# A transformer block on one core: all softmax denominators of the second half's queries summed on GpSimd, and the ones product of the sum as a step of its own

## The chip, the cores and the metric

The kernel runs on one core of one Trainium2 chip. The metric is the device time of one execution in microseconds. Engines are named as in the profile: PE is TensorE's matmul side and PEld its weight loads, DVE is VectorE, ACT is ScalarE, POOL is GpSimd, SP is SyncE, which here issues all transfers.

## What is computed

Input x is 4 batches of 1024 tokens with 128 features, all float32. Three layers follow each other:

```python
x = x + 0.5 * ffn(layernorm(x))      # 8 experts of 128x128, the two best by a router, weighted
x = x + attention(layernorm(x))
x = x + 0.5 * ffn(layernorm(x))

# attention: 8 query heads of 128, 2 key/value heads (4 query heads share one), causal
q = (x @ wq).reshape(B, T, 2, 4, 128)
k_lat, v_lat = x @ wk_down, x @ wv_down        # 32 wide for each key/value head
k, v = k_lat @ wk_up, v_lat @ wv_up
scores = q.k * 128**-0.5, masked to key <= query
y = softmax(scores) @ v
return y.reshape(B, T, 1024) @ wo
```

## The kernel before

**Tiling.** A batch has two chunks of 512 tokens (c = 0, 1) and eight tiles of 128 (j = 0 to 7). The attention works in *quads*: one chunk of queries and one key/value head g with its four query heads. There are 16 quads in all, Q = 4b + 2c + g. A quad with c = 0 has key tiles 0 to 3, one with c = 1 (the second half's queries) has key tiles 0 to 7. The up projections of keys and values are folded into the queries and into `wo`, so keys and values are 32 wide.

**The steps of a quad.** (1) `maximum` (M): scores in the query by key layout, from which VectorE takes each query's maximum (`reduce`), merged, transposed (R) and added to the stacked queries as two rows by SP's transfers. (2) `scores` (S): for each of the quad's *slots* (26 of 512 columns where c = 1, 10 where c = 0) the scores in key by query layout, the causal squares masked by a small bf16 product; two banks take turns. (3) `exponent` (E, on ACT, L739) turns the bank into weights in `prob`, a ring of 16 slots. (4) `weighted_values` (V, L1257): one step for each key tile, four heads, each onto 32 partitions of the bank OB, f32 (two matmul instructions each, so eight in the trace). (5) The denominators: the same weights times `ones` [128 x 32] (L1262) into a second bank.

**Widths.** Where key tile j lies on the diagonal (j >= 4c), only queries from `first_query(q, j)` = (j - 4c) * 128 on see it. So for c = 1 tiles 0 to 4 are 512 queries wide, tile 5 is 384, tile 6 is 256 and tile 7 is 128. Tiles 5 and 7 share four slots (384 + 128 columns), and tile 6 has two slots with two heads each. `ORDER[q]` gives the tiles in the order in which their weights come: 0, 1, 2, 3, 4, 5, 7, 6.

**Who sums what.** In c = 1 quads the tiles of `summed(q)`, 0 to 4, have no ones product of their own. GpSimd adds their weights into `sums` (`add_weights`, L620): for each pair of heads, tile 1 to tile 0, then tiles 2, 3, 4 onto it, eight adds of 2 x 512 elements a partition. The tiles of `direct(q)`, 5 to 7, and all tiles of c = 0 quads get ones products on PE. The last values step (tile 6) waits for the quad's adds and does the ones product of `sums` as well (L1268), into the same bank. A slot of `prob` may be overwritten when its values step is done and, for summed tiles, its add too (`exponent`).

**After a quad.** VectorE transposes the denominators, takes the reciprocal and spreads it (`denominators`, L995 to L1002); ACT copies OB to `o_sb` (`output`); GpSimd multiplies (`normalise`, L607, POOL's Y); when a chunk's two quads are through, PE multiplies by `wo` (`join`, J, L1279), VectorE adds x, and the layer norm and the last ffn of this chunk can begin. `o_sb`, `r_t` and OB exist once, so quads pass through there one after the other.

**The other work.** The experts (`expert_products`, Y on PE, L1165 to L1167) fill PE between attention steps; ACT and VectorE weigh them (L704, L947) and GpSimd adds up (`finish_tile`, three operations a tile, POOL's F, L591 to L598). GpSimd also takes the layer norm's -0.5 power (L574) and the shift (L578), POOL's N, n and m, each after seven small VectorE operations (`statistics`, L861).

**What sets the order.** Each engine's program is a written list: `PE_ORDER`, `DVE_ORDER`, `ACT_ORDER`, `POOL_ORDER`, `SP_ORDER`, one letter a step. A step waits for its semaphores with everything behind it. A digit behind a PE letter is the PSUM bank that the step takes; `take` waits until the bank's former content has been read. The end of both lists before, for PE and for POOL:

```python
    "Sl7Y0VSSY1SY5SSY6VSSY0SY7SVSSY1SY5SVSSSSSV2VVY3Y2Y6J0JJJz7l1Y0Y5Y2Y3Y6Y7Y1Y0"       # PE
    "FFFFFAAAAAAFAFAFFYmmYYAAAAAAAAmmFFFFFFFFFYFFFFFFAFAFFAAAAAAFFFFFFYFFFFFFmmFFFFFFFFFFFFFFFFFF"   # POOL
```

## Time and profile before

| what | us |
|---|---|
| median of 3 runs (512.12 to 513.83) | 512.28 |
| the profiled execution | 512.54 |
| its span, first to last instruction | 510.8 |
| PE busy | 462.2 |
| DVE busy | 415.8 |
| ACT busy | 336.8 |
| POOL busy | 302.2 |
| mean granted clock of PE, share of full speed | 0.954 |

The profiled execution is 0.26 us above the median, and 1.7 us of it lie around the span. In the profile a matmul's end is modelled and busy times of neighbours overlap, so the time from one start to the next tells better what a step costs PE. A note in brackets behind a timeline row is the idle time of the engine before it and what ended it.

### The profile page before, as it was taken

What the parts mean: (1) busy time and instruction counts of PE and PEld (TensorE: products, weight loads), DVE (VectorE), ACT (ScalarE), POOL (GpSimd) and SP (SyncE); (2) the same over time, 40 slices, a digit from 0 to 9 for tenths busy, and PEclk for the clock granted to TensorE, in tenths of its full rate; (3) what the DMA queues carried; (4) which work ended last, traced back from release to release, by engine and by line L of the source; (5) the groups of instructions that cost most, each with busy time, mean ns of one, the idle gap of its engine ahead of it and who ended that gap; (6) DMA issues with size and microseconds to landing.
All of it is one profiled execution on the core that took longest, in us unless ns stands there. A gap on an engine that the chain in (4) does not pass through costs nothing.

```text
span 510.8 us, 9871 instructions
## 1 busy us (share of the span) xinstructions
PE 462.2 (90%) x3166; PEld 251.1 (49%) x3166; DVE 415.8 (81%) x1320; ACT 336.8 (66%) x748; POOL 302.2 (59%) x323
## 2 busy tenths in 40 slices
PE   1896989998699999999999999999999999899752
PEld 1673535453254446464645664555534545454441
DVE  6787789989976988989969999988888877863454
ACT  3356417667359767797787976677776496788523
POOL 4166006209745940598489737298498129889835
PEclk9995967999889999999999999999999999999967
DMA  7001310002001010002110100210101000000000
GB/s 199 16 22 42 88 48 22 1 2 81 19 2 32 18 33 2 1 1 58 23 57 13 53 1 2 48 33 17 53 2 54 1 1 2 1 23 1 22 21 21
DMA packets 21123, 14.50 MB, mean 28 GB/s; under 512 B 2952, under 2 KB 20944, under 8 KB 21072
## 3 DMA queue, kind: packets, MB, share of 16 engines
q1 hardware_dynamic: 21072, 13.88, 10.6%
q8 instruction: 25, 0.41, 0.3%
q14 instruction: 26, 0.21, 0.2%
HBM read 3.78 MB, written 2.10 MB: 11 GB/s over the span
## 4 chain that ended last, share of the span: by engine, by line
PE 70%; DVE 14%; ACT 6%; issue 5%; POOL 2%; DMA 2%; SPq 1%; ACTq 0%; POOLq 0%; DVEq 0%
PE bank L1257 12%; PE bank L1235 11%; PE bank L1212 11%; PE bank L1165 6%; PE bank L1262 5%; PE bank L1166 5%; PE bank L1167 5%; DVE diff L861 3%; PE bank L1240 2%; PE bank L1183 2%; ACT prob L739 2%; ACT xn L675 2%; PE bank L1279 2%; DMA x<-in_L_attn_x 2%; PE bank L1152 1%
## 5 line engine op out<-in xcount | busy, mean ns | idle before, releaser
L739 ACT ACTIVATE prob<-bank,exp_scale 128x512 f32<-128x512 f32 x288 | 188.6, 690 | 61.2 <-PE bank L1240 33.1
L620 POOL TENSOR_TENSOR sums<-sums,prob 128x1024 f32<-128x1024 f32 x48 | 112.3, 2371 | 9.5 <-ACT prob L739 9.5
L1212 PE MATMUL bank<-k_stack,q_stack 96*128 96x512 f16 (+3 forms) x384 | 101.2, 336 | 8.5 <-DVE m_part L963 5.4
L1235 PE MATMUL bank<-q_stack,k_stack 98*128 98x512 f16 (+3 forms) x384 | 105.3, 330 | 2.0 <-ACT prob L739 1.5
L704 ACT ACTIVATE scaled<-bank,gate 128x128 f32<-128x128 f32 x256 | 75.3, 374 | 28.7 <-POOL x L598 10.5
L591 POOL TENSOR_TENSOR pair_sum<-dve_sum,scaled 128x256 f32<-128x256 f32 x64 | 46.7, 730 | 80.2 <-DVE dve_sum L947 66.7
L967 DVE TENSOR_REDUCE m_part<-bank 128x1 f32<-128x512 f32 x128 | 83.4, 679 | 7.0 <-PE bank L1212 6.4
L963 DVE CUSTOM_DVE_ANT_0 masked<-bank,mask_qk 128x384 f32<-128x384 f32 (+1 forms) x128 | 75.1, 617 | 8.5 <-PE bank L1212 8.3
L1257 PE MATMUL bank<-prob,v_lat 128*32 128x512 f32 (+3 forms) x768 | 81.8, 500 | 0.1
L1165 PE MATMUL bank<-we_hi,xT_hi 128*128 128x512 f32 x128 | 66.8, 522 | 1.6 <-DVE m_part L963 1.6
L1235 PEld LDWEIGHTS bank<-q_stack,k_stack 98*128 98x128 f16 x384 | 33.4, 98 | 64.7 <-ACT prob L739 32.0
L1212 PEld LDWEIGHTS bank<-k_stack,q_stack 96*128 96x128 f16 x384 | 33.6, 100 | 51.9 <-issue 13.5
L1166 PE MATMUL bank<-we_lo,xT_hi 128*128 128x512 f32 x128 | 53.6, 419 | 0.0
L1167 PE MATMUL bank<-we_hi,xT_lo 128*128 128x512 f32 x128 | 53.4, 417 | 0.0
L607 POOL TENSOR_TENSOR yT<-o_sb,r_t 128x512 f32<-128x512 f32 x16 | 20.4, 1277 | 51.8 <-DVE r_t L1002 49.7
L675 ACT ACTIVATE xn<-x,shift,rstd 128x128 f32<-128x128 f32 x96 | 40.8, 489 | 10.6 <-POOL shift L578 10.6
L620 POOL TENSOR_TENSOR sums<-prob 128x1024 f32<-128x1024 f32 x16 | 37.8, 2366 | 13.2 <-ACT prob L739 13.2
L574 POOL TENSOR_TENSOR rstd<-var_eps,half_power 128x4 f32<-128x4 f32 (+1 forms) x18 | 22.0, 1225 | 38.6 <-DVE neg_mean L861 38.6
L947 DVE SCALAR_TENSOR_TENSOR dve_sum<-bank,gate,scaled 128x128 f32<-128x128 f32 x128 | 39.7, 342 | 6.3 <-ACT scaled L704 6.1
L1240 PE MATMUL bank<-mask_kq,ident_b 128*128 128x256 bf16 (+1 forms) x160 | 40.4, 252 | 0.0
L1262 PE MATMUL bank<-prob,ones 128*32 128x384 f32 (+3 forms) x448 | 37.9, 410 | 0.0
L1165 PEld LDWEIGHTS bank<-we_hi,xT_hi 128*128 128x128 f32 x128 | 26.1, 204 | 17.5 <-issue 5.6
(128 smaller groups left out, 722.8 us busy)
## 6 DMA issues: line engine op xcount, KB each, us to landing
q_stack<-q_hi SPq DMA_DIRECT2D x32, 128.0 KB, 3.2
x<-in_L_attn_x SPq DMA_DIRECT2D x8, 256.0 KB, 3.0
q_stack<-q_lo SPq DMA_DIRECT2D x16, 128.0 KB, 3.2
out_x<-x SPq DMA_DIRECT2D x8, 256.0 KB, 2.3
k_stack<-k_hi SPq DMA_DIRECT2D x16, 64.0 KB, 2.1
we<-in_L_ffn_expert_weights SPq DMA_DIRECT2D x1, 512.0 KB, 4.0
x<-in_L_attn_wq SPq DMA_DIRECT2D x1, 512.0 KB, 6.6
x<-in_L_attn_wo SPq DMA_DIRECT2D x1, 512.0 KB, 7.9
```

The costliest lines, as they stand in the source:

```text
L620: nc.gpsimd.tensor_tensor(into, first if j == 1 else into, new, ALU.add).then_inc(sum_step, 1)
L704: nc.scalar.activation(scaled[:, tile % NTB, i, :], home_of(("y", f, n, 2 * t))[:, i * D:(i + 1) * D], ACT.Copy, scale=gate_of(f, n, t)[:, ...
L739: nc.scalar.activation(prob[:, n % NP, :], bank[ST + n % NST][:], ACT.Exp, scale=exp_scale[:, 0:1]).then_inc(p_ready, 1)
L963: V.tensor_tensor_reduce(out=masked[:, m % 2, 0:w], in0=seen[:, 0:w], in1=mask_qk[:, CH - w:CH], op0=ALU.add, op1=ALU.max, scale=1.0, scal ...
L967: V.reduce_max(into, seen[:, 0:w], AX.X).then_inc(mx_red, 1)
L1165: mm(into[:], hi, we_hi[:, cols(half)], start=True, stop=False)
L1166: mm(into[:], hi, we_lo[:, cols(half)], start=False, stop=False)
L1167: mm(into[:], lo, we_hi[:, cols(half)], start=False, stop=True).then_inc(y_done, 1)
L1212: last = mm(into[:, n * w:(n + 1) * w], q_stack[0:MROW, c, g * NR + r, (i % TC) * P:(i % TC + 1) * P], k_stack[0:MROW, b % 2, g, k:k + w], ...
L1235: last = mm(into[:, at:at + CH - off], k_stack[:, b % 2, g, j * P:(j + 1) * P], q_stack[:, c, g * NR + r, off:CH], start=at == 0, stop=not ...
L1257: last = mm(bank[OB][r * DL:(r + 1) * DL, off:CH], v_lat[:, b % 2, j, g, :], weights[r], start=first, stop=final, skip_group_check=True)
L1262: last = mm(sums_to[r * DL:(r + 1) * DL, off:CH], ones[:], weights[r], start=j == direct(q)[0], stop=final and not summed(q), skip_group_c ...
```

## The change

1. `summed(q)` gives all eight tiles of a c = 1 quad, in the order 0, 1, 2, 3, 4, 5, 7, 6; `direct` goes. GpSimd does six adds more in each of these eight quads, two for each of tiles 5, 7 and 6, as narrow as the tile: 2 x 384, 2 x 128 and 2 x 256 elements a partition. The tiles' ones products go: 12 of them a quad, 24 matmul instructions.
2. The ones product of the sum leaves the last values step. It becomes `sum_products`, step D of `PE_ORDER`, takes the denominator bank itself and raises a new semaphore, `den_done`. VectorE's transpose waits for that in c = 1 quads, and the first add of a quad waits for it in the place of `pv_done` before it overwrites `sums`.
3. The weights slots of tiles 5, 6 and 7 are now also held until their adds are done (`exponent` is unchanged but asks `summed`).
4. All five order lists are new. They hold the same steps, but for POOL's 112 A in the place of 64, and PE's eight D.

```diff
 def summed(q):
-    c, g = QUADS[q]
-    return list(range(c * TC + 1)) if c else []
-
-def direct(q):
-    return [j for j in ORDER[q] if j not in summed(q)]
+    return ORDER[q] if QUADS[q][0] else []
+
+def quads_summed(Q):
+    return sum(QUADS[i % NQ][0] for i in range(Q + 1))
...
 def sum_done(b, q, j, pair):
-    return sum_count(b * NQ + q) - 2 * len(summed(q)[1:]) + 2 * (max(j, 1) - 1) + pair + 1
+    return sum_count(b * NQ + q) - 2 * len(summed(q)[1:]) + 2 * (max(summed(q).index(j), 1) - 1) + pair + 1
...
 PE_ORDER = steps(
...
-    "Sl7Y0VSSY1SY5SSY6VSSY0SY7SVSSY1SY5SVSSSSSV2VVY3Y2Y6J0JJJz7l1Y0Y5Y2Y3Y6Y7Y1Y0"
...
+    "M0SM6M5SM1SM7SM0SV6SSVSJ5M1SM7VSM0SVSJSM1VVSR7JSVSSVSSJSSVSSJ0SSJVVSVJSSJSSVSSz6Sz1Y7l5lY0SVY6SSY1SSVSSz5Y7Y"
+    "0SY6SSVSSY1SVY5SSY7SY0SVVY1Y6SY2Y3Y7Vl5Y0D1Y6Y2Y1Y3Y7Y5Y0D6J6JJJz2l1Y6Y3Y5Y7Y0Y2Y1Y6"
 POOL_ORDER = (
...
-    "FFFFFAAAAAAFAFAFFYmmYYAAAAAAAAmmFFFFFFFFFYFFFFFFAFAFFAAAAAAFFFFFFYFFFFFFmmFFFFFFFFFFFFFFFFFF"
...
+    "nAAAAAAAAAAAFAAFFAFFFAFFFFFAFFAAFYFAFAFFAFAAAFAFAFAFFAYYAAAAAAYAmAmAAAAmAAmAAAAFAAFFFFFAFFFFAFFFFFAFAFAFFFAFA"
+    "AYFFFYFFFFFFmmFFFFFFFFFFFFFFFFFF"
...
+    "D": [("den", Q) for Q in range(NB * NQ) if QUADS[Q % NQ][0]],
...
             def add_weights(b, q, j, pair):
-                Q, g = b * NQ + q, QUADS[q][1]
-                heads = slice(2 * pair, 2 * pair + 2)
-                new, first = (prob[:, at % NP:at % NP + 2, :] for at in
-                              (b * NS + QSTART[q] + weights_at(q, i)[2 * pair][0] for i in (j, 0)))
-                into = sums[:, g, heads, :]
-                pool.wait_ge(p_ready, b * NS + QSTART[q] + weights_at(q, j)[2 * pair + 1][0] + 1)
+                g, off = QUADS[q][1], first_query(q, j)
+                slots = [(b * NS + QSTART[q] + i, at) for i, at in weights_at(q, j)[2 * pair:2 * pair + 2]]
+                (one, at), (two, beside) = slots
+                new = prob[:, one % NP:one % NP + 2, at:at + CH - off] if two > one else \
+                    prob[:, one % NP, :].rearrange("p (h q) -> p h q", h=2)
+                first = (b * NS + QSTART[q] + 2 * pair) % NP
+                first = prob[:, first:first + 2, :]
+                into = sums[:, g, 2 * pair:2 * pair + 2, off:CH]
+                pool.wait_ge(p_ready, two + 1)
                 if j == 1 and pair == 0:
-                    need(pool, pv_done, (GROUP[b - 1, q, ORDER[q][-1]] + 1) if b else 0)
+                    need(pool, den_done, quads_summed(b * NQ + q - NQ) if b else 0)
...
                     b, q = divmod(Q, NQ)
-                    dve.wait_ge(pv_done, GROUP[b, q, ORDER[q][-1]] + 1)
+                    if summed(q):
+                        dve.wait_ge(den_done, quads_summed(Q))
+                    else:
+                        dve.wait_ge(pv_done, GROUP[b, q, ORDER[q][-1]] + 1)
...
-                sums_to = take(("den", b * NQ + q)) if j == direct(q)[0] else home_of(("den", b * NQ + q))
-                if j not in summed(q):
+                if not summed(q):
+                    sums_to = take(("den", b * NQ + q)) if first else home_of(("den", b * NQ + q))
                     for r in range(NR):
                         last = mm(sums_to[r * DL:(r + 1) * DL, off:CH], ones[:], weights[r],
-                                  start=j == direct(q)[0],
-                                  stop=final and not summed(q), skip_group_check=True)
-                if final and summed(q):
-                    pe.wait_ge(sum_step, sum_count(b * NQ + q))
-                    for r in range(NR):
-                        last = mm(sums_to[r * DL:(r + 1) * DL, :], ones[:], sums[:, g, r, :],
-                                  start=False, stop=True, skip_group_check=True)
+                                  start=first, stop=final, skip_group_check=True)
                 last.then_inc(pv_done, 1)
+
+            def sum_products(Q):
+
+                into = take(("den", Q))
+                pe.wait_ge(sum_step, sum_count(Q))
+                for r in range(NR):
+                    last = mm(into[r * DL:(r + 1) * DL, :], ones[:], sums[:, Q % NKV, r, :],
+                              start=True, stop=True, skip_group_check=True)
+                last.then_inc(den_done, 1)
```

## Rows read from the trace of the kernel before

**Rows 1.** The page's part 1: busy time, share of the span, instructions.

```profile
PE 462.2 (90%) x3166; PEld 251.1 (49%) x3166; DVE 415.8 (81%) x1320; ACT 336.8 (66%) x748; POOL 302.2 (59%) x323
```

**Rows 2.** Windows: stretch, its length, each engine's busy us, granted clock, DMA share, GB/s.

```profile
118.00:150.00 32.00, 26.27 (x157) 12.28 (x161) 31.15 (x73) 16.50 (x28) 23.09 (x13) 0.89 0.15 39
200.00:300.00 100.00, 99.74 (x700) 55.99 (x698) 87.81 (x287) 80.30 (x186) 73.79 (x77) 1.00 0.11 27
300.00:420.00 120.00, 119.58 (x938) 61.80 (x936) 104.28 (x292) 85.21 (x177) 69.35 (x65) 1.00 0.09 22
422.54:481.04 58.50, 55.51 (x389) 28.69 (x388) 35.67 (x126) 43.55 (x97) 53.98 (x45) 1.00 0.03 7
```

**Rows 3.** Groups by form, GpSimd: count, busy us, mean ns, idle before and its releasers.

```profile
L620 POOL TENSOR_TENSOR sums<-sums,prob 128x1024 f32<-128x1024 f32 x48 | 112.3, 2371 | 9.5 <-ACT prob L739 9.5
L591 POOL TENSOR_TENSOR pair_sum<-dve_sum,scaled 128x256 f32<-128x256 f32 x64 | 46.7, 730 | 80.2 <-DVE dve_sum L947 66.7 <-PE bank L1070 8.7 <-DVE x L1008 4.7
...
L607 POOL TENSOR_TENSOR yT<-o_sb,r_t 128x512 f32<-128x512 f32 x16 | 20.4, 1277 | 51.8 <-DVE r_t L1002 49.7 <-issue 2.1
...
L574 POOL TENSOR_TENSOR rstd<-var_eps,half_power 128x8 f32<-128x8 f32 x6 | 9.8, 1642 | 15.8 <-DVE neg_mean L861 15.8
...
L578 POOL TENSOR_TENSOR shift<-neg_mean,rstd 128x8 f32<-128x8 f32 x6 | 1.2, 204 | 0.5
```

**Rows 4.** Timeline, GpSimd, last two quads: start us, length us, operation, count.

```profile
422.54 4.72 POOL L620 TENSOR_TENSOR sums<-prob 128x1024 f32<-128x1024 f32 x2 [0.36 <-ACT prob L739]
427.21 14.01 POOL L620 TENSOR_TENSOR sums<-sums,prob 128x1024 f32<-128x1024 f32 x6
...
479.76 1.28 POOL L607 TENSOR_TENSOR yT<-o_sb,r_t 128x512 f32<-128x512 f32 x1
```

**Rows 5.** The chain that ended last, from 476 us: start us, length us, piece.

```profile
476.95 0.90 PE bank L1268 x8
...
481.18 2.04 PE bank L1279 x16
```

**Rows 6.** Timeline, PE, end of quad 11: values (L1257) and ones products (L1262, L1268).

```profile
389.18 0.83 PE L1262 MATMUL bank<-prob,ones 128*32 128x384 f32 x8
389.94 0.39 PE L1235 MATMUL bank<-q_stack,k_stack 98*128 98x512 f16 x1
...
392.58 0.40 PE L1262 MATMUL bank<-prob,ones 128*32 128x128 f32 x8
392.92 0.61 PE L1212 MATMUL bank<-k_stack,q_stack 96*128 96x512 f16 x2
...
393.78 0.64 PE L1257 MATMUL bank<-prob,v_lat 128*32 128x256 f32 x8
394.24 0.61 PE L1262 MATMUL bank<-prob,ones 128*32 128x256 f32 x8
394.67 1.04 PE L1268 MATMUL bank<-sums,ones 128*32 128x512 f32 x8
395.64 0.39 PE L1212 MATMUL bank<-k_stack,q_stack 96*128 96x512 f16 x1
```

**Rows 7.** The same chain near 455 us: a 512 wide values step by itself.

```profile
455.48 0.99 PE bank L1257 x8
```

**Rows 8.** Timeline, PE: the scores of quad 14's slot 5.

```profile
420.87 0.39 PE L1235 MATMUL bank<-q_stack,k_stack 98*128 98x512 f16 x1
```

**Rows 9.** VectorE's statistics (min/median/max ns, then timeline rows), and a PE wait.

```profile
L861 DVE TENSOR_TENSOR diff<-stats x18: 153/166/2283, 6.8 to 485.1; 128x4 f32<-128x4 f32 x12, 128x8 f32<-128x8 f32 x6
...
122.69 2.28 DVE L861 TENSOR_TENSOR diff<-stats 128x4 f32<-128x4 f32 x1
...
136.46 2.19 DVE L861 TENSOR_TENSOR diff<-diff 128x8 f32<-128x8 f32 x1
...
438.96 2.29 DVE L861 TENSOR_TENSOR diff<-diff 128x4 f32<-128x4 f32 x1
...
139.77 0.61 PE L1212 MATMUL bank<-k_stack,q_stack 96*128 96x256 f16 x2 [3.56 <-DVE m_part L963]
```

74 lines of the change are left out of this document (39 added, 35 removed).

## The prediction

> **What bounds the kernel now.** I read the page's busy shares first: TensorE 90% of the span, VectorE 81%, GpSimd 59% [rows 1]. The reader should see an engine with little room (PE) from which the change takes work, and one with room on average (GpSimd) that gets it. An average hides stages, so next come the windows [rows 2]. From 200 to 420 us PE is busy 99.7% of the time at the full clock while GpSimd is at 74% and then 58%. From 118 to 150 PE is busy only 26.3 of 32 us and VectorE 31.15. In the last attention stretch, 422.54 to 481.04, PE has 55.5 busy of 58.5 us, but GpSimd 54.0: there the two engines are nearly level. Third I read GpSimd's operations by form, GpSimd's timeline in that stretch [rows 3, 4] and the chain behind it [rows 5].
>
> I number the 16 quads (batch b, quad q) as Q = 4b + q; the eight with summed tiles are 2, 3, 6, 7, 10, 11, 14 and 15, with key tiles 0 to 7 taken in the order 0 to 5, 7, 6.
>
> **Removed from PE.** The ones products of tiles 5, 7 and 6 in each of the eight quads. From start to start in the timeline, for the 384 wide tile: 389.18 to 389.94 less the 0.1 of switching to the next form, 0.67 us. For the 128 wide tile 392.58 to 392.92 less the same 0.1, 0.24. For the 256 wide tile 394.24 to 394.67, 0.43 [rows 6]. That is 1.34 a quad, 10.7 us in all. The other bound is 1.8, if I took the busy times in those rows (0.83, 0.40, 0.61), which overlap their neighbours.
>
> **The ones product of the sum.** It moves out of the last values step into a step of its own. Behind other f32 work it takes 0.97 with the switch (394.67 to 395.64 [rows 6]), about 0.86 marginal; alone it should look like a values step of the same shape alone, 0.99 [rows 7]. Extra 0.13 x 8 = 1.0 us. PE's net saving is 9.7 us. The denominator bank is now taken at that step and not at tile 5, so it is held shorter; no row shows a PE wait on it before, so I cost this at nothing, between -1 and 0. The new semaphore is waited for by VectorE's transpose. Queued behind it on VectorE are the steps of its order; for quad 15 these are four combining steps and the join, which need it anyway.
>
> **Added to GpSimd.** 48 adds: 16 each of 768, 512 and 256 elements a partition. The 1024 element add takes 2371 ns; the products at 512 and 256 elements take 1277 and 730 [rows 3]. The line between 1277 and 2371 gives 1.82 us for 768. So 1.82 + 1.28 + 0.73, twice a quad, 7.66 us a quad and 61 us in all: GpSimd goes from 302 to 363 us busy. Bounds for the twelve narrow adds in the last two quads: 12 x 0.73 = 8.8 us, were they all at the price of the narrowest of them, which would end the kernel at 509.1; and 12 x 2.37 = 28 us, were narrow as dear as wide, 528. I take 15.3, since the rows have two of the three widths themselves and both neighbours of the third; for the same reason the upper end stays outside my range.
>
> **Where the lag is covered.** The final ones product used to need tile 4's add; now it needs tile 6's. Counted in the new order at the prices above, PE has 7.6 to 16 us of other steps between a quad's last values step and its new step in quads 2 to 11 and 32 us in quad 14: as much as the 7.66 us or more. A weights slot (16 of them) is now also held until its narrow tile is added. At these distances that costs little, and I put nothing on it. This holds while GpSimd has no backlog.
>
> **Moved steps.** ACT's, VectorE's and SP's lists hold what they held, reordered by a few places to fit PE's new list. SP's transfers of keys, queries and maxima stay ahead of the scores that need them; their cover is the same full PE as before, so I cost them at nothing, and at a few us on either side if a list is badly fitted, which the range has room for.
>
> **The last two quads decide.** GpSimd's queue there is a fixed list. Before, it runs from the first add of quad 14 at 422.54 to the end of quad 15's multiplication at 479.76 + 1.28 = 481.04 [rows 4], 58.5 us, of which 54.0 busy [rows 2]; of the other 4.5 us some 1.2 are short gaps between dependent operations and 3.3 are waits. Right behind it comes the last join, at 481.18, and from there to the end 29.6 us which both versions have in the same order on all engines [rows 5].
>
> The new list from quad 14's first add to quad 15's multiplication holds the same 16 wide adds, eight tile endings, quad 14's multiplication and its normalisation pair, and more: twelve narrow adds (15.3), quad 13's multiplication (1.28 [rows 3]) and the normalisation pair of an eight tile run (1.64 + 0.20 [rows 3]). That is 18.4 us more. The 54.0 busy us become 72.4. The 1.2 of gaps stay. Of the 3.3 of waits, those for VectorE's combining should shrink in a backlog, so I keep 2.0 of 3.3: 75.6 us.
>
> When can it start? Its first add needs the weights of quad 14's slots 4 and 5; before, slot 5's scores are issued at 420.87 [rows 8]. The new PE order reaches that slot with less done: six quads' savings (6 x 1.34 - 6 x 0.13 = 7.3 us), four join tiles fewer (16 matmuls are 2.04 us [rows 5], so a tile of four is 0.51; 2.0), and quad 13's four values steps with their ones products: 1.84 + 1.43 + 0.99 + 0.58 = 4.8 us, with the values part taken as dear as the ones part (393.78 to 394.24 is 0.46 against 0.43) and 0.1 of switching in each [rows 6, 7]. One step of transposes fewer and three maxima blocks more (some 0.2 each) about cancel; I take off 0.3. Sum 13.8 us, if PE stays full up to there as it is now. Start 422.5 - 13.8 = 408.7.
>
> End of quad 15's multiplication: 408.7 + 75.6 = 484.3 against 481.04. So the last join moves 3.3 us later and so does the end. The profiled execution took 512.54 with a span of 510.8 and stands 0.26 above the median 512.28. It goes to 515.8, the median to **515.6 us**.
>
> PE, meanwhile, would reach the last ones product at about 470 (join at 474.2 below, less 3.3 and 1.0) and the last narrow add ends only at 484.3 - 4.3 = 480. The 9.7 us saved, and the few us of PE steps put ahead, become a wait of some 10 us on GpSimd.
>
> **A rule against the change.** The small VectorE operations of the normalisation statistics take 0.17 us in the median and 2.28 at most; one at 438.96 took 2.29, to 441.25, where the last of eight adds in a row ends (427.21 + 14.01 = 441.22) [rows 4, 9]. Five such, the first at 122.69 and the last at 136.46, lie where VectorE is full and PE waits 3.56 us at 139.77 [rows 2, 9]. The Trainium skill, SBUF — State Buffer, section "SBUF: two separate sides", says that a VectorE operation with two SBUF inputs or in a two port mode and a GpSimd one shut each other out for the whole instruction. The trace agrees: 2.28 against 0.16. What it would give here is the third rival, priced from rows.
>
> **Rivals.**
> (1) PE sets the end (faster). Join at 481.18 - 9.7, plus 2.7, since before three expert steps covered most of the 3.3 us from sum product to join and the new order has none there: 474.2, so 505.3 us. It needs GpSimd's list 10 us shorter than I count, which only nearly free narrow adds would give. Against it: widths 256 and 512 are in the rows.
> (2) The early stall goes (faster). In the new order the second of the two statistics runs of 122 to 139 stands behind the maxima of quad 3, and the first run's power stands after three adds and not eight, so no more than three of its operations can meet one. If the five blocked operations (10.5 us against 0.8 free) no longer hold PE, all starts up to 9.7 us sooner: 515.6 - 9.7 = 506; half of it 511. Against: both runs still lie beside adds, and there are more of these.
> (3) VectorE's blocked operations hold up GpSimd (slower). The new order puts two statistics runs inside quad 14's adds, each followed by a GpSimd power that waits for it. Four of seven operations in a run have blocked before; if all do, a run takes up to 4 x 2.3 us and not 0.7. The adds they wait for are work that must be done anyway; only what remains after the add ahead of the power is lost, 2 to 3 us a run. It decides when a run begins less than four adds ahead of its power: 520 to 521 us.
> (4) GpSimd never idles and nothing changes upstream (no change): 408.7 + 72.4 + 1.2 is 482.3, 1.3 us later, 513.5 us.
> (5) The change does no less on PE than it says: the 96 matmuls are gone by construction; I give this no chance.
>
> **How the numbers follow.** Forecast 0.38 (514 to 518), rival 4 with its neighbours 0.24, rival 3 0.17, rival 2 0.13, rival 1 0.08. Predicted 515.6. Leaving out the far halves of rivals 1 and 2 (0.1) and what lies past rival 3 (0.1): 507.0 to 521.0. A measurement of this kernel can tell about 0.5% from no change, 2.6 us: faster is under 509.7, slower over 514.8. Faster takes rival 1 and most of rival 2 (and combinations of it with rival 4), 0.20. The forecast lies just over the upper bound, so a quarter of it falls inside, with rival 4 and the weaker half of rival 2: 0.35. Slower 0.45.
>
> **What would show it.** Right: PE busy near 450 us; GpSimd near 363; the adds of 768, 512 and 256 at 1.8, 1.3 and 0.7; in quads 2 to 11 hardly a wait at the new ones step; quad 14's first add near 409; GpSimd about 97% busy from there; PE waiting some 10 us in all for GpSimd before the last two ones steps; the last join near 484.5. Wrong: a first add of quad 14 before 405 (rivals 1, 2), narrow adds under 0.6 each, or new PE waits ahead of 400 us, which would make it slower than I say. Long statistics operations at 415 to 435 with GpSimd idle at its power mean rival 3.

## The result and the profile after

The changed kernel takes 523.76 us (median of 4 runs, 522.85 to 527.25) against 512.2 us for the kernel before on the same chip: a ratio of 1.024, with a 95% interval of 1.019 to 1.029. The forecast was 515.6 with a range of 507.0 to 521.0. The direction was the likeliest one, the time lies 8 us above the forecast and outside the range. The profiled execution took 523.50 with a span of 521.6, where that of before had 510.8.

The page's part 1 of the changed kernel (busy time, share of the span, instructions) answers to [rows 1]:

```profile
PE 461.0 (88%) x2974; PEld 244.7 (47%) x2974; DVE 415.2 (80%) x1320; ACT 336.3 (64%) x748; POOL 359.9 (69%) x371
```

GpSimd's 359.9 is the 363 that was forecast. TensorE lost 192 matmuls, but its busy time fell by 1.2 us only, where "near 450" was forecast. What runs at the lower clock counts for more (eight matmuls of a ones product 1.94 us there and 1.04 at the full clock, below), and the mean granted clock went from 0.954 to 0.933. The windows of the changed kernel (stretch, length, busy us of PE, PEld, DVE, ACT, POOL, granted clock) answer to [rows 2]; the last is GpSimd's stretch from quad 14's first add to quad 15's multiplication:

```profile
118.00:150.00 32.00, 26.63 (x152) 11.98 (x150) 30.05 (x69) 18.40 (x32) 26.73 (x17) 0.89 0.15 39
200.00:300.00 100.00, 99.17 (x654) 53.33 (x654) 86.49 (x276) 80.38 (x184) 84.83 (x83) 1.00 0.10 27
300.00:420.00 120.00, 118.92 (x871) 58.68 (x869) 106.00 (x302) 84.87 (x177) 91.17 (x85) 1.00 0.09 22
414.70:491.05 76.35, 64.77 (x427) 32.90 (x419) 41.55 (x142) 47.97 (x107) 71.54 (x60) 0.96 0.03 8
```

From 200 to 420 TensorE is full, as before, and GpSimd has taken up its adds. In the last stretch both engines have gaps now: TensorE 64.8 busy of 76.35 us, at a granted clock of 0.96 where it was 1.00.

GpSimd's operations by form (count, busy us, mean ns, idle time ahead) answer to [rows 3]:

```profile
L625 POOL TENSOR_TENSOR sums<-sums,prob 128x1024 f32<-128x1024 f32 x48 | 112.8, 2367 | 7.4 <-ACT prob L744 7.3
...
L625 POOL TENSOR_TENSOR sums<-sums,prob 128x768 f32<-128x768 f32 x16 | 28.9, 1821 | 0.0
...
L625 POOL TENSOR_TENSOR sums<-sums,prob 128x512 f32<-128x512 f32 x16 | 20.2, 1276 | 0.0
...
L625 POOL TENSOR_TENSOR sums<-sums,prob 128x256 f32<-128x256 f32 x16 | 11.4, 727 | 0.0
```

The three widths cost 1.82, 1.28 and 0.73 us, each as forecast. GpSimd's timeline around the last two quads (start, length, operation) answers to [rows 4]:

```profile
399.88 1.27 POOL L625 TENSOR_TENSOR sums<-sums,prob 128x512 f32<-128x512 f32 x1
409.14 1.27 POOL L609 TENSOR_TENSOR yT<-o_sb,r_t 128x512 f32<-128x512 f32 x1 [7.99 <-DVE r_t L1010]
412.61 1.27 POOL L609 TENSOR_TENSOR yT<-o_sb,r_t 128x512 f32<-128x512 f32 x1 [2.19 <-DVE r_t L1010]
414.70 2.36 POOL L625 TENSOR_TENSOR sums<-prob 128x1024 f32<-128x1024 f32 x1 [0.82 <-ACT prob L744]
...
483.32 2.52 POOL L625 TENSOR_TENSOR sums<-sums,prob 128x512 f32<-128x512 f32 x2
485.80 1.29 POOL L609 TENSOR_TENSOR yT<-o_sb,r_t 128x512 f32<-128x512 f32 x1
...
489.79 1.26 POOL L609 TENSOR_TENSOR yT<-o_sb,r_t 128x512 f32<-128x512 f32 x1 [0.94 <-DVE r_t L1010]
```

Two things are to be seen. The stretch runs from 414.70 to 491.05, 76.35 us, where 75.6 were forecast (GpSimd is busy 94% of it, not 97%); but it begins 6.0 us later than the forecast 408.7. And just ahead of it GpSimd stands idle for 8.0 and 2.2 us: quad 11's last add ends at 401.15, and that quad's multiplication waits for VectorE's reciprocals of a ones product that stands at 405.1 in TensorE's list. That multiplication came at 398.1 before. The first add of quad 14 itself waited 0.82 us for its weights, not for this.

At the end, TensorE's timeline shows the last ones product and the wait for the last multiplication:

```profile
485.49 0.48 PE L1174 MATMUL bank<-we_lo,xT_hi 128*128 128x512 f32 x1
...
486.82 1.07 PE L1278 MATMUL bank<-sums,ones 128*32 128x512 f32 x8
491.19 2.56 PE L1289 MATMUL bank<-wo_lat,yT 128*128 128x128 f32 x16 [3.31 <-POOL yT L609]
```

The last narrow add ends at 485.8 and the ones product of its sum starts at 486.82, right behind an expert product that had itself come late. The trace alone does not say which of the two held it.

**A table for all kernels.** To place the loss I priced every step of TensorE's list at its start-to-start time in full stretches (0.99 for a 512 wide values step, 0.81 for an expert product and so on) and took the sum of the prices from the time. What is left is time in which TensorE waited, ran at the lower clock, or took longer over its steps than their prices say; the column alone does not tell these apart. "Quad 2" is from its first scores to its last values step, "to 14" from there to the scores of quad 14's slot 5, "last" from those to the last join. "Work" is the price of all steps up to the last join, "start" what was lost before quad 2 (loading, preparation; 40.5 to 47.9 by chance). All numbers in us, medians aside from one profile each; the profiled execution of e11 took 3.3 us and that of e15 3.9 us more than the median beside it. The profile of e5 is from a slow execution (574.09 us; the median of its three fast ones is 569.3), so its row is used for the places of the waits and not for single us.

```
              median  start  quad 2  to 14   last   work   last join
before        512.2    43.0    9.9    0.0     4.1   424.2   481.2
change        523.76   43.7   11.6    3.7    17.4   414.8   491.2
e1            520.75   44.3    6.2    4.2    17.9   414.8   487.3
e2            525.94   43.2   10.3    4.2    20.1   414.8   492.5
e3            524.32   45.2   10.4    4.4    18.9   414.8   493.7
e4            509.11   40.8    1.2    7.6     4.1   424.2   477.9
e5            571.43   44.9   12.1   45.6    24.4   414.8   541.7
e6            513.49   42.1    9.9    4.8     8.4   414.8   480.0
e7            536.95   40.5   12.9   22.3     5.5   421.3   502.6
e8            523.49   41.5    1.2   22.1     5.6   421.3   491.8
e9            524.04   44.4   11.5    4.5    15.9   414.8   491.1
e10           523.37   43.4   11.5    4.4    17.3   414.8   491.3
e11           506.62   44.7    1.2    0.6     5.5   425.3   477.3
e12           512.71   41.0    1.2   14.0     3.9   422.6   482.7
e13           524.09   44.1   11.5   15.1     7.2   414.8   492.8
e14           522.31   42.8   11.5   14.7     3.8   417.4   490.2
e15           518.08   47.9    1.7    4.7    20.0   414.8   489.0
e16           513.28   43.1    1.7   15.2     3.8   417.4   481.3
e17           505.95   44.3    1.7    6.2     3.9   418.7   474.8
```

Change against before: the work fell by 9.4 (9.7 were forecast), the start cost 0.7 more, quad 2 1.7, the stretch to quad 14 3.7, the last one 13.3. That makes the last join 10.0 us later; the end behind it took 30.4 instead of 29.6.

Two windows check the 3.7 of the long middle stretch, from the end of quad 2's values to the scores of quad 14's slot 5, before (first fence) and after:

```profile
151.56:420.87 269.31, 268.13 (x2010) 140.90 (x2002) 232.19 (x691) 202.78 (x434) 169.15 (x161) 1.00 0.10 24
```

```profile
155.32:413.50 258.18, 256.22 (x1785) 130.10 (x1785) 226.31 (x677) 195.73 (x420) 205.19 (x191) 1.00 0.10 25
```

TensorE stands idle for 2.0 us there instead of 1.2, at the full clock in both. So only 0.8 of the 3.7 us is waiting. In the other 2.9 TensorE was busy: the steps of the new order took that much longer than their prices. Which steps do, no run shows.

### The profile page after: what moved, and what is told of

Read it like the earlier page. It is cut to its first block, busy times and chain, and to the rows that moved or that the text cites. A ratio compares the mean times of both kernels' runs of the same rounds, so it can differ in the third digit from the quotient of the medians.

```text
span 521.6 us, 9633 instructions
## 1 busy us (share of the span) xinstructions
PE 461.0 (88%) x2974; PEld 244.7 (47%) x2974; DVE 415.2 (80%) x1320; ACT 336.3 (64%) x748; POOL 359.9 (69%) x371
## 4 chain that ended last, share of the span: by engine, by line
PE 56%; DVE 14%; POOL 11%; issue 10%; ACT 5%; DMA 2%; SPq 1%; POOLq 0%; ACTq 0%; DVEq 0%
PE bank L1264 10%; PE bank L1243 10%; PE bank L1220 9%; POOL sums L625 6%; PE bank L1173 4%; PE bank L1174 3%; PE bank L1175 3%; PE bank L1269 2%; PE bank L1248 2%; DVE dve_sum L952 2%; DVE diff L866 2%; PE bank L1191 2%; ACT xn L680 2%; PE bank L1289 2%; ACT prob L744 2%
## 5 line engine op out<-in xcount | busy, mean ns | idle before, releaser
L625 POOL TENSOR_TENSOR sums<-sums,prob 128x1024 f32<-128x1024 f32 (+3 forms) x96 | 172.9, 1821 | 7.4 <-ACT prob L744 7.3
L1220 PE MATMUL bank<-k_stack,q_stack 96*128 96x512 f16 (+3 forms) x384 | 103.3, 336 | 7.6 <-DVE m_part L972 3.9
L1243 PE MATMUL bank<-q_stack,k_stack 98*128 98x512 f16 (+3 forms) x384 | 106.5, 333 | 1.9 <-ACT prob L744 1.0
L709 ACT ACTIVATE scaled<-bank,gate 128x128 f32<-128x128 f32 x256 | 75.4, 373 | 44.2 <-POOL x L600 17.4
L680 ACT ACTIVATE xn<-x,shift,rstd 128x128 f32<-128x128 f32 x96 | 40.9, 488 | 11.6 <-POOL shift L580 11.6
L625 POOL TENSOR_TENSOR sums<-prob 128x1024 f32<-128x1024 f32 x16 | 37.8, 2365 | 12.9 <-ACT prob L744 12.9
L1248 PE MATMUL bank<-mask_kq,ident_b 128*128 128x256 bf16 (+1 forms) x160 | 40.5, 253 | 0.0
L1173 PEld LDWEIGHTS bank<-we_hi,xT_hi 128*128 128x128 f32 x128 | 26.6, 208 | 25.8 <-ACT scaled L709 5.8
L952 DVE SCALAR_TENSOR_TENSOR dve_sum<-bank,gate,x 128x128 f32<-128x128 f32 x64 | 22.0, 344 | 15.0 <-PE bank L1175 10.0
```

Of the source, the lines that this page charges most:

```text
L625: nc.gpsimd.tensor_tensor(into, first if j == 1 else into, new, ALU.add).then_inc(sum_step, 1)
L709: nc.scalar.activation(scaled[:, tile % NTB, i, :], home_of(("y", f, n, 2 * t))[:, i * D:(i + 1) * D], ACT.Copy, scale=gate_of(f, n, t)[:, ...
L952: V.scalar_tensor_tensor(out=sums[e % 3], in0=home_of(("y", f, n, 2 * t + 1))[:, e * D:(e + 1) * D], scalar=gate_of(f, n, t)[:, HALF + e:H ...
L1173: mm(into[:], hi, we_hi[:, cols(half)], start=True, stop=False)
L1220: last = mm(into[:, n * w:(n + 1) * w], q_stack[0:MROW, c, g * NR + r, (i % TC) * P:(i % TC + 1) * P], k_stack[0:MROW, b % 2, g, k:k + w], ...
L1243: last = mm(into[:, at:at + CH - off], k_stack[:, b % 2, g, j * P:(j + 1) * P], q_stack[:, c, g * NR + r, off:CH], start=at == 0, stop=not ...
```

## The experiments

Ratios are against the kernel before on the same chip, whose median lay between 511.3 and 513.4 in the groups.

**e1 and e2: are the narrow adds what costs?** Both keep every list of the change and cut narrow adds to one column: all 48 (e1), or the 12 of the last batch (e2). The other columns of these tiles are left out of the sums.

```diff
+                if off:                      # e2: if off and b == NB - 1:
+                    into, new = into[:, :, 0:1], new[:, :, 0:1]
                 nc.gpsimd.tensor_tensor(into, first if j == 1 else into, new, ALU.add).then_inc(sum_step, 1)
```

> The changed kernel, but each of GpSimd's 48 narrow adds works on one column of two heads only (part of the denominators is left out); lists, waits and PE's work stay. Theory A (GpSimd's queue in the last two quads sets the end): twelve adds of 15.3 us in all there become some 2.4, the stretch from quad 14's first add to quad 15's multiplication goes from 76.4 to about 63.5 us, and the kernel from 523.8 to about 511; a little less, 509, if the 36 earlier narrow adds cost something too. Theory B (the new lists are slow by themselves, whatever the adds cost): the time stays above 520.

> The same, but only in the last batch (quads 14 and 15), twelve of the 48 narrow adds (part of those denominators is left out). Theory A: all of the gain of the first run is here, about 511, within 1 us of it, since the 36 earlier narrow adds lie behind PE's work. If the earlier ones hold PE or VectorE up, this run stays 2 us or more above the first. Theory B: above 520.

e1 took 520.75 (ratio 1.015, 1.008 to 1.022) and e2 525.94 (1.024, 1.015 to 1.033). An add of one column takes 0.20 us, so e1 takes 52 us of work from GpSimd and e2 12.9, and the kernel gets 3 us and nothing. Both stay above 520, as theory B says. GpSimd's timeline in e2, at the end:

```profile
479.42 1.27 POOL L609 TENSOR_TENSOR yT<-o_sb,r_t 128x512 f32<-128x512 f32 x1
483.17 0.73 POOL L593 TENSOR_TENSOR pair_sum<-dve_sum,scaled 128x256 f32<-128x256 f32 x1 [2.48 <-DVE dve_sum L954]
...
491.11 1.26 POOL L609 TENSOR_TENSOR yT<-o_sb,r_t 128x512 f32<-128x512 f32 x1 [6.15 <-DVE r_t L1012]
```

The adds are through at 479.4, and the last ones product still starts at 487.28. Behind the GpSimd queue that I had counted stands a second chain that ends at nearly the same time: expert products 116 to 119 of the new list, whose banks come free by VectorE's combining, ScalarE's scaling and GpSimd's tile endings in turn. In TensorE's timeline of e2 they follow a wait and run at the lower clock (0.63 instead of 0.39 us a matmul):

```profile
483.14 0.79 PE L1175 MATMUL bank<-we_hi,xT_hi 128*128 128x512 f32 x1 [1.91 <-DVE dve_sum L954]
483.73 0.63 PE L1176 MATMUL bank<-we_lo,xT_hi 128*128 128x512 f32 x1
...
487.28 1.94 PE L1280 MATMUL bank<-sums,ones 128*32 128x512 f32 x8
```

What e1 gains over the change lies in quad 2 (6.2 us lost instead of 11.6), ahead of all of this.

**e3: does the early part of the lists matter?** The first 114 of TensorE's steps, and the same part of the other lists, in the order of the kernel before.

```diff
 PE_ORDER = steps(
-    first 114 steps of the change
+    first 114 steps of the kernel before
     the rest of the change
```

> The changed kernel with the early part of all five lists (up to about 98 us, before any quad with summed tiles) taken from the kernel before. In the profiles the first scores start at 87.0 us after and 83.6 before, with 0.8 us less PE work in front of them. Theory A1 (the early part of the new lists is slower): the time falls by about 4 us, to 520. Theory A2 (the early difference is the chance of the clock in one execution): 523.8, within 1 us.

524.32 (1.021, 1.013 to 1.030): no difference, as theory A2 says: the early lists are not what costs. The start column differs by up to 7 us between single profiles.

**e4: what do VectorE's blocked operations cost before?** The kernel before, with the two statistics runs and their powers ahead of quad 2's adds.

```diff
-nnYFFFFFFYAAAAAAAAnnNNY      (GpSimd; VectorE likewise)
+nnYFFFFFFYnnNNAAAAAAAAY
```

> The kernel before, all computed; only the two runs of small statistics operations that met quad 2's adds (122 to 142 us) stand now ahead of these adds on VectorE, and their powers ahead of the adds on GpSimd. Theory C (the operations blocked by adds, five of 10.5 us in all, are what costs PE some 10 us between 118 and 149): the blocked ones go and the time falls by 5 to 9 us, to 503 to 507. Rival (VectorE's own work in that stretch is the bound and blocked time is slack): less than 2 us.

509.11 (0.995, 0.992 to 0.999), 2.8 us under before: less than the 5 to 9 of theory C, more than the rival's 2. The loss in quad 2 falls from 9.9 to 1.2 us, but 7.6 are lost in the next stretch, where none was before. The first part of that is plain in its TensorE timeline: the last ones product, still inside the values step, now waits for GpSimd's eighth add, and runs at half speed behind the wait.

```profile
140.42 0.61 PE L1262 MATMUL bank<-prob,ones 128*32 128x256 f32 x8
144.17 1.93 PE L1268 MATMUL bank<-sums,ones 128*32 128x512 f32 x8 [3.13 <-POOL sums L620]
```

**e5 and e6: the change in the old order.** All eight quads as in the change, the lists of the kernel before; narrow adds behind the wide ones; the new step 2 to 5 us behind the values step (e5), or directly behind it, with adds of one column (e6).

```diff
-   ... V5 ... V SSL6SM0 ...                 (before: tile 5 takes the bank, tile 6 holds the sum product)
+   ... V  ... V SSL6SM0Sx1S D5 ...          (e5)
+   ... V  ... V D5 SSL6SM0 ...              (e6)
```

> All eight quads as in the change (tiles 5, 7 and 6 added by GpSimd, ones product of the sum as a step of its own), but in the order of the kernel before on every engine: the narrow adds stand behind the wide ones, the new step 2 to 5 us of PE steps behind the last values step, the transposes and the multiplication moved with it. Theory L (the new lists themselves lose the time in the last quads; with the old order only GpSimd's queue is left): quad 14's first add at 416 to 418 (eight us saved, some four of waits at the new step of quads 2, 3 and 11), GpSimd's stretch 54.0 + 15.3 + 2.5 = 72 us, last join near 489, kernel 516 to 521. Rival N (the narrow adds slow everything wherever they stand): 524 or more, as the change. Which of the two engines holds the end is told by this run only together with the one that has one column.

> The same old order with every narrow add cut to its first column (the other columns of the sums are left out) and the new step directly behind the last values step: PE's saving with next to nothing added to GpSimd. To be held against the run with the new lists and one column, 520.75 us. Theory L: the saving of 10.7 less 1.0 comes through where PE is full: 511.9 - 9.7 = 502, at most 506 if VectorE holds quads 2 and 3. Rival P (PE's saving is not worth time, since other engines set the pace as soon as PE has room): 509 or more. If it is under 507, the 14 us to the run with the new lists are what the lists cost.

e5 took 571.43 (1.112, 1.101 to 1.123), rival N's side (524 or more) and far above it. e6 took 513.49 (1.004, 1.000 to 1.008), on rival P's side: even with adds next to free, taking 9.4 us of work from TensorE brings nothing, though part of this is the place of the new step (1.9 us of waiting at quad 2, 2.0 at quad 15, and 2.2 at the last join, behind which the clock is down). In the full stretches less than half of the saving is there (slot 5 of quad 14 comes 3.1 us sooner), the last values step comes 4.6 us sooner, the last join 1.2. In e5, 45.6 us go on the way to quad 14: at the new steps of quads 7, 10 and 11 (4.2, 5.4 and 4.8 us of waiting), in a wait of 6.8 us for VectorE's maxima at 200 us, and elsewhere. The pair shows one thing more: in the last stretch the old order loses 8.4 us with one column and 24.4 with whole adds. The difference, 16.0, is near the 15.3 of the prediction, though the new step's place differs between the two as well. In the new order that stretch loses 17.9 (e1) and 20.1 (e2) with adds of one column and 17.4 with whole ones.

**e7, e8 and e12: narrow adds only where GpSimd has room.** Old order; quads 6, 7 and 10 (e7), the same with statistics first (e8), or 6 and 10 alone with the new step 5 to 7 us behind (e12, which also has e11's step, below).

```diff
+NARROW = (6, 7, 10)                          # e12: (6, 10)
 def summed(Q):
-    return ORDER[q] if QUADS[q][0] else []
+    return (ORDER[Q % NQ] if Q in NARROW else list(range(c * TC + 1))) if c else []
```

> The old order, and only quads 6, 7 and 10 have their narrow tiles added by GpSimd (in the stretch in which PE is full and GpSimd at 58 to 74%); all else as before. Theory L: three times 1.34 less 0.13 is 3.6 us off PE, nothing in the last two quads changes, so all of it comes through: 508.3 us. Rival N: GpSimd's 23 us of adds delay the tile endings behind them and these PE: 512 or more.

> The run before it in this group, with the statistics and powers ahead of quad 2's adds (509.1 us by itself) and quad 2's ones product of the sum as a step 5 us later. If the two gains add: 509.1 - 3.6 = 505.5; with the wait of 4 us at quad 2's sum gone too, down to 502. If VectorE holds quads 2 and 3 anyway, 505 to 506.

> The run before it in this group, and GpSimd also adds the narrow tiles of quads 6 and 10, whose join waits for the next quad anyway; their ones product of the sum stands 5 to 7 us behind the last values step, the adds behind the values steps of their tiles. TensorE saves 2 times 1.21 us. Theory W (where nothing waits for the sum, the saving comes through): 1 to 2.4 us below the run before it, near 501.5. Rival N (each narrow quad costs more in tile endings held up on GpSimd than it saves): 3 us or more above it.

536.95 (1.050, 1.042 to 1.058), 523.49 (1.023, 1.016 to 1.030) and 512.71 (1.001, 0.998 to 1.005): misses of 29, 18 and 11 us, and rival N's side in e7 and e12. TensorE's timeline of e7 at quad 7 shows how a step that saves 1.2 us loses some 6:

```profile
302.74 1.50 PE L1272 MATMUL bank<-prob,v_lat 128*32 128x384 f32 x24
308.45 1.94 PE L1287 MATMUL bank<-sums,ones 128*32 128x512 f32 x8 [4.21 <-POOL sums L633]
310.32 0.61 PE L1251 MATMUL bank<-q_stack,k_stack 98*128 98x512 f16 x1
```

The sum is ready 4.2 us behind the end of the last values step, TensorE waits that long, and what follows runs at the lower clock (1.94 us for eight matmuls that take 1.04 in [rows 6], 0.61 for scores that take 0.39). Room on GpSimd on average is not room right behind a quad's last scores. In the change's own lists, with the step 8.1 to 16.4 us behind, TensorE waits for no sum in quads 2 to 11.

e12 shows a second way. Its ones product of quad 10 waits, and not for its own sum:

```profile
364.39 1.93 PE L1286 MATMUL bank<-sums,ones 128*32 128x512 f32 x8 [3.81 <-ACT scaled L716]
```

Its bank was that of an expert product, which ScalarE had still to scale. That scaling (363.19) waited 2.82 us for a tile ending of GpSimd, and the tile ending stood behind four narrow adds (357.44 to 361.34). This is rival N's mechanism.

**e9 and e10: a late router step?** In e2 the gates of the second last chunk seemed to hold expert products 116 to 119. Its router step moved 5.5 us forward, on top of e2 (e9) and of the change (e10).

```diff
-VVY1Y6SY2Y3Y7Vl5Y0D1Y6
+VVl1Y6SY5Y2Y3Y7VY0D1Y6
```

> The change with the narrow adds of the last batch cut to one column (as in the run that gave 525.94 us), and beside it the router step of the second last chunk 5.5 us earlier: on TensorE at 468 instead of 474, its 27 gate steps on VectorE from 470 on, between the combining steps, its exponential on ScalarE ahead of tile 54's scaling (tiles 107 and 108 of the expert products take the banks that it gave up). Theory R (two things hold the last join at the same place: GpSimd's adds to 485.8, and the gates that come too late for expert products 116 to 119): with both gone the last ones product starts near 482 instead of 487.3 and the last join near 487 instead of 492.5, the kernel 519 to 521 against 525.9. Rival G (only GpSimd's queue counts): nothing changes, 525 to 527.

> The change itself, whole narrow adds, with the same earlier router step. Theory R: GpSimd's last narrow add still ends near 485.8, so the last ones product stays there and the last join comes at most 1 us sooner: 522.5 to 524 us. If the router step alone were the bound, it would gain 4 to 5 us, 519.

524.04 (1.023, 1.017 to 1.030) and 523.37 (1.024, 1.016 to 1.032). e10 lies where theory R has it. e9, which decides, lies between the two theories: the gain of 5 us didn't come. The ones product of quad 14 now starts at 480.5 and 479.4, where it was at 475.8 in the change. In e9:

```profile
480.47 1.07 PE L1280 MATMUL bank<-sums,ones 128*32 128x512 f32 x8 [1.55 <-DVE gate L905]
```

It takes bank 1, and the moved router step had been given that bank too, so it waits for VectorE's gate steps: a wait of the edit's own making (1.55 us in e9, 3.1 in e10). Behind it TensorE runs through its expert products without a wait and at the full clock (0.39 us a matmul, where e2 had 0.63), and the last ones product starts at 486.7, as ever. So moving this step gains nothing; whether the late gates would be the bound with another bank, the pair does not tell.

**e11: the other half of the change by itself.** e4, and only quad 2's ones product of the sum as a step of its own, behind ten other steps. No narrow adds.

```diff
-V(tile 6, with the sum product) SSL6SM0Sx1
+V SSL6SM0Sx1 D
```

> None of the narrow adds; only the other half of the change, used once: the kernel before with the statistics and powers ahead of quad 2's adds (509.1 us) and quad 2's ones product of the sum as a step of its own, 10 to 11 places after its last values step, so that TensorE does not stand 4.2 us at 140 us until GpSimd's last wide add. The other ones products of sums stand directly behind their values. In the run with three narrow quads the offset at quad 4 was 44.6 us with this and 50.5 without it. Theory S (that wait and the lower clock after it are what the earlier statistics lost again): 503 to 504 us. Rival V (VectorE sets the pace of quads 2 and 3 anyway and takes the gain back later): 507 to 509.

506.62 (0.991, 0.987 to 0.995). The 7.6 us that e4 lost again are 0.6 now, which speaks for theory S; the time is 2.6 above its 504 and 0.4 under rival V's 507.

**e13 and e14: is it the order of the last batch?** The change's lists up to quad 11's ones product (406 us), the old order from there. In e13 the last batch's narrow adds have one column, as in e2; in e14 quads 14 and 15 are as before.

```diff
-NARROW: all eight                            # e13, narrow adds of batch 3 one column
+NARROW = (2, 3, 6, 7, 10, 11)                # e14
 PE_ORDER: the change up to ...M1SM7SM0SD5, then VVJ5JJJR5M7SM0V6SM1M5... as before
```

> The change's order on every engine up to 406 us (quad 11's ones product of the sum), and from there the order of the kernel before (joins of chunk 5 at once, routers of chunks 4 and 5 ahead of quad 14's adds); the narrow adds of the last batch cut to one column, as in the run that gave 525.94 us with the new order. Theory O (the new order of the last batch is itself what takes 13 us there): the last join at 478 to 482 instead of 492.5, the kernel 508 to 512. Rival E (the new order is late only because of what lies ahead of it; another order finds the same waits): 520 or more.

> The same mixed order; GpSimd adds narrow tiles in the first three batches only, whole, and quads 14 and 15 are as in the kernel before, nothing left out. Theory O: TensorE keeps its saving of six quads, GpSimd has 58.5 us in the last two quads as before. From the offset of 59 at quad 14 (52.9 before) and 4.1 us lost after it: last join near 480.5, the kernel 509 to 511, within 0.5 percent of before. Rival E: 518 or more.

524.09 (1.024, 1.019 to 1.029) and 522.31 (1.018, 1.011 to 1.026). Both times are rival E's. But the last stretch does lose less, 7.2 and 3.8 us instead of 17 to 20; 11 more are lost just ahead, where the joins of chunk 5 come. They lie at the place where the two orders meet. The spliced list has the join's four steps in a row, two values steps behind quad 11's ones product. In the change the join ends up 13 us behind that product and in the kernel before 6 us, and neither waits there. In e14 TensorE waits 2.3 us for the multiplication ahead of that join, 0.8 behind it and 3.5 for ScalarE's copy of the output. So these two runs lose their time to a place that neither order has.

**e15: statistics first, in the change.**

```diff
-FFFFFFAAAnnAAAAAAAAAAAAAANYAAAFFFAFFFAFFFAAAAAANYY     (GpSimd; VectorE likewise)
+FFFFFFnnNNAAAAAAAAAAAAAAAAAYAAAFFFAFFFAFFFAAAAAAYY
```

> The change itself with both statistics runs of quads 2 and 3 and their two powers ahead of quad 2's adds, as in the run of the kernel before that gave 509.1 us. Theory B (VectorE's small operations shut out by GpSimd's adds, which now last longer, lose 11.5 us between 119 and 155 us in the change): quad 14 and the end come 6 to 9 us sooner, 515 to 518 us. Rival N (what is gained is taken back by the next wait, as in the kernel before): 521 to 523.

518.08 (1.012, 1.006 to 1.019). Theory B's side, at its upper end. The loss in quad 2 falls from 11.6 to 1.7 us; 1.0 more is lost on the way to quad 14 (4.7 instead of 3.7), and 2.6 more in the last stretch. VectorE's timeline, the same operation in the change and in e15:

```profile
123.10 2.19 DVE L866 TENSOR_TENSOR diff<-diff 128x4 f32<-128x4 f32 x1
...
125.80 1.80 DVE L866 TENSOR_SCALAR diff<-diff 128x4 f32<-128x4 f32 x1
```

```profile
126.91 0.16 DVE L866 TENSOR_TENSOR diff<-diff 128x4 f32<-128x4 f32 x1
...
127.31 0.17 DVE L866 TENSOR_SCALAR diff<-diff 128x4 f32<-128x4 f32 x1
```

In e15's window from 118 to 150 TensorE is busy 31.3 of 32 us at the full clock; in the change it was 26.6 at 0.89:

```profile
118.00:150.00 32.00, 31.30 (x213) 15.63 (x212) 27.69 (x85) 24.88 (x46) 24.57 (x19) 1.00 0.16 41
```

**e16 and e17: quad 11.** e16 is e14 with statistics first. e17 differs from it in three things at once: quad 11's narrow tiles go back to TensorE, its ones product stands 2.0 us behind the last values step, and the old order begins there, so that the four steps of the join are no longer in a row and stand some 9 us behind that product.

```diff
-NARROW = (2, 3, 6, 7, 10, 11)
+NARROW = (2, 3, 6, 7, 10)
-   ... SM5SM1SM7M0SD5VVJ5JJJR5M7SM0V6SM1 ...
+   ... M0V6VVY7SM1SDW6M0M5SM1 ... M1M7J5SJJM0JM1M7M0 ...
```

> The run with narrow adds in the first three batches only, and the statistics first as well; nothing left out. Theories O and B together: 509 to 511 less 6 to 9, so 501 to 504 us, under the best so far (506.6). If B falls, 507 to 510.

> As the run with narrow adds in the first three batches and the statistics first (513.28 us), except quad 11: its narrow tiles go back to TensorE, its ones product of the sum comes 2 us behind its last values step, at 391 instead of 406 on that clock, and the old order begins there. Nothing is left out. Theory J (the late sum of quad 11, by its multiplication and join, holds up the routers and expert tiles of the last batch): the 10 us lost between 397 and 414 us go, TensorE has 1.2 us more to do: 503 to 506 us. Rival X (the loss comes from the splice or from the last batch itself): 511 us or more.

e16 took 513.28 (1.004, 1.000 to 1.007), 9 us above the upper end of what I expected of it; e17 505.95 (0.989, 0.985 to 0.993), as expected of theory J. GpSimd's timelines of e16 (first fence) and e17, around quad 11's multiplication:

```profile
390.37 1.27 POOL L633 TENSOR_TENSOR sums<-sums,prob 128x512 f32<-128x512 f32 x1
398.88 1.26 POOL L617 TENSOR_TENSOR yT<-o_sb,r_t 128x512 f32<-128x512 f32 x1 [7.23 <-DVE r_t L1018]
407.08 1.65 POOL L584 TENSOR_TENSOR rstd<-var_eps,half_power 128x8 f32<-128x8 f32 x1 [6.94 <-DVE neg_mean L874]
```

```profile
387.36 0.46 POOL L608 TENSOR_TENSOR x<-pair_sum,dve_sum 128x128 f32<-128x128 f32 x1
387.93 1.27 POOL L617 TENSOR_TENSOR yT<-o_sb,r_t 128x512 f32<-128x512 f32 x1
```

And the window from 395 to 425 us, e16 first: TensorE busy 22.5 of 30 us at a clock of 0.83, against 29.85 at 1.00.

```profile
395.00:425.00 30.00, 22.50 (x184) 11.54 (x183) 16.16 (x41) 13.66 (x27) 8.08 (x7) 0.83 0.01 2
```

```profile
395.00:425.00 30.00, 29.85 (x259) 16.04 (x258) 24.02 (x64) 22.46 (x41) 13.33 (x8) 1.00 0.01 2
```

Quad 11 is the second half of its chunk: its multiplication releases the join, the join the statistics, routers and gates of the expert tiles that follow. With the multiplication 11 us later (398.9 against 387.9), TensorE has too little other work in e16's list there. Its timeline has the join and what comes behind it:

```profile
400.28 3.65 PE L1298 MATMUL bank<-wo_lat,yT 128*128 128x128 f32 x16 [2.26 <-POOL yT L617]
404.72 0.28 PE L1215 MATMUL bank<-ident,m_fin 128*16 128x128 f32 x1 [0.79 <-DVE x L1024]
...
410.07 1.93 PE L1272 MATMUL bank<-prob,v_lat 128*32 128x512 f32 x8 [4.30 <-ACT o_sb L651]
```

The pair rules out the last batch's old order as the cause. It does not part the late sum from the splice: e16's list, with the join close behind the ones product, is worse than the change's own, in which TensorE is busy 29.5 of the 30 us from 395 to 425.

## Why the prediction was wrong

**What held.** The work taken from TensorE, at the prices of single steps: 9.4 us against 9.7. The prices of the adds and GpSimd's total (359.9 against 363). The length of the last stretch, 76.35 against 75.6, agrees too, but in part by luck: e2 takes 12.9 us of GpSimd's work out of it and the last join comes no sooner, so GpSimd's queue alone does not set it. Rival 3 did not come: in the whole kernel seven of the small VectorE operations took over 1 us, 11.3 us in all, where before seven took 14.6; in both kernels two of the seven lie beside quad 14's adds, and GpSimd waits 1.4 us for the statistics in the last stretch of either.

**The step that failed: the start, "sum 13.8 us, if PE stays full up to there as it is now. Start 408.7".** It came at 414.7. The work up to there was less by 13.5 us at the prices of single steps, so the count was right, but the time did not follow it. Of the 6.1 us lost, 0.7 fall to the start of the profile, 1.7 to quad 2 and 3.7 to the stretch from there to quad 14. In quad 2 the condition failed: TensorE lost 11.6 us there, where it had lost 9.9. In the long stretch it nearly held, with 0.8 us more of idle time, and the sum itself promised too much: 2.9 us went into steps that took longer in the new order than their prices. The adds are not the reason, since with one column that stretch loses 4.2 as well (e1); what is stays open. By the prediction's own sum the rest follows: 6.0 from the start, 0.8 from the stretch, 0.8 from the end make 7.6 of the 7.7 us between the forecast's 515.8 and the profiled 523.5.

**A second step was wrong without showing in the sum: "PE, meanwhile, would reach the last ones product at about 470" and then wait some 10 us for GpSimd.** TensorE had expert products left until 486.8. The prediction took GpSimd's queue as the only bound in the last stretch; e1, e2 and e9 show that the new lists lose 16 to 20 us there with the adds next to free; the old order loses 8.4 so (e6). I had counted the new order's steps, and not the chain on which the deferred ones hang (join of chunk 5, which is the second chunk of batch 2; statistics, router, gates, three engines in turn for each expert tile). "Moved steps ... I cost them at nothing" is where this belongs: the joins of chunk 5 begin at 417.9 instead of 401.0, their routers stand at 445 and 446 instead of 422 and 427.

**Where the lag was costed at nothing.** "PE has 7.6 to 16 us of other steps between a quad's last values step and its new step ... I put nothing on it." For TensorE this held: it waits for no sum in quads 2 to 11. But the step is late by as much for who waits behind it. For quad 11 that is the join of its chunk. Between e16 and e17 lie 7.3 us, with 1.2 us of TensorE work more in the better one, where the saving of a quad is 1.2 us. These 7.3 us hold the late sum and the splice together, as said above. For the change's own lists, which spread the delay otherwise, it was not tried, and how their 13.3 us divide between this delay and the rest stays open.

**Rivals 1 and 2.** Rival 1 gave 505 if the narrow adds were nearly free. Made nearly free they end the kernel at 513.5 in the old order (e6) and at 520.8 in the new one (e1), so it was priced too low as well. Rival 2 saw the right place. With the statistics out of the adds' way (e15) the change gets 5.7 us faster; it named 9.7 at most. In the change as it is the stall only grew, from 9.9 to 11.6 us.

**The ladder.** From the change, step by step: statistics first 518.1; the last batch as before, with the old order behind quad 11, 513.3; quad 11 as before 506.0. And without any narrow add, but with statistics first and quad 2's step in a place of its own, 506.6. What the two fastest kernels (1.1 and 0.9 percent under before) share is the freed stretch at quad 2, and quad 2's ones product of the sum as a step of its own. The narrow adds that e17 keeps take 6.6 us of work from TensorE, and its time can't be told from e11's, which has none; the two differ in their lists as well.

## What to carry to other kernels

When work moves from the full engine to one with room, ask when its result is due, not only how long it takes. A step that saved 1.2 us cost some 6 where it stood too close behind its sum (e7), and nothing was waited for where it stood 8 us or more behind. Where an order is written out by hand, count the chain of the deferred steps as well as the steps: here the adds could be made next to free and the new order still ended no more than 3 us sooner (e1, e2). Price the steps in the order in which they will stand, and not only those taken out. And look first for the stall that is already there: taking 14 small operations out of the way of GpSimd's adds gained 3 to 9 us (e4, e15, e16 against e14), where the whole transfer gained none.

## What the runs showed of the hardware

**TensorE's clock makes short waits dear.** Behind waits of 2.2 to 4.2 us the same operations take up to 1.9 times as long: eight matmuls of a ones product 1.04 us in [rows 6], 1.94 in e7 and 1.93 in e4; the sixteen of the last join 2.04 in [rows 5], 2.56 in the change, 3.59 in e6 behind a wait of 2.17:

```profile
479.96 3.59 PE L1300 MATMUL bank<-wo_lat,yT 128*128 128x128 f32 x16 [2.17 <-POOL yT L617]
```

The granted clock of the last stretch fell from 1.00 to 0.96. Between the two levels, 1.2 and 2.4 GHz, that is 8% of the stretch or 6 us at the lower one, and up to 3 us lost by it. The Trainium skill, TensorE: Matmul & The Clock Gate, section "What's actually happening", has it that the lower clock is the default and that activity releases it. These rows agree.

**Small VectorE operations are held up beside GpSimd's adds.** In the change the small VectorE operations with two inputs from SBUF, and TENSOR_SCALAR with one, took up to 2.19 us beside adds of 2.37 us, and 0.16 to 0.17 in e15 away from them. The Trainium skill, SBUF — State Buffer, section "SBUF: two separate sides", has the rule for a VectorE operation with two SBUF inputs and for one in a two port mode. The rows agree for two inputs. TENSOR_SCALAR with one source of 4 elements was held for 1.80 us as well; in which mode it ran, no row shows.
